# Feed-forward and output products in two 64-row parts, each beside a part of the next

## The chip, the core and the metric

One NeuronCore of a Trainium2 chip runs the whole program. Its engines work side by side and wait for each other by semaphores: TensorE (PE; its weight loads are listed as PEld), VectorE (DVE), ScalarE (ACT), GpSimdE (POOL) and the DMA queues (SP and ACT issue them here). TensorE's results land in eight PSUM banks of 128 partitions by 512 floats. The metric is the device time of one execution in microseconds (us); shown is the median of a few runs.

## What is computed

Eight sequences of 512 tokens, width 256, go through two layers:

```python
# layer 0: gated feed-forward with quantised activations and weights
h = x * (scale * rsqrt(mean(x*x) + EPS));  u = h @ up_w.T
val, gate = split(u);  h = val * gelu(gate)
x = act_quant(h) @ weight_quant(down_w).T + x
# layer 1: 16-head attention (16 wide), then SwiGLU with 1024 hidden columns;
# norm(x) = gamma * x * rsqrt(mean(x*x) + EPS) + beta
q, k, v = (norm(x) @ w.T for w in (W_q, W_k, W_v))
x = x + a_alpha * (softmax(q @ k.T / 4) @ v) @ W_o.T
y = silu(norm(x) @ gate_w.T) * (norm(x) @ hidden_w.T)
out = x + f_alpha * (y @ out_w.T + out_b)
```

## The kernel before

Phase 1 (to about 254 us) is layer 0, tile by tile. Phase 2 is layer 1, sequence by sequence ("batch" 0 to 7), and a tail finishes the last sequence. The change touches phase 2 alone.

A float32 product is made of three products of rounded parts, `PARTS = ((0, 0), (0, 1), (1, 0))`: high by high, high by low, low by high. So a feed-forward product of 128 hidden columns (`gate` f or `hidden` f, f from 0 to 7) takes 3 x 2 = 6 matmuls, since the model width is two row blocks of 128. An output piece (t, half) takes 12 matmuls of 256 columns: token tile t, one half of the sum over f.

Each batch has `HALVES` = 32 steps `h`. For each, `pe_batch` issues an excursion (`excursion_pe`): two scores (L1059) and, for a later group of heads, two raw products (L976), whose row maxima VectorE takes (L1009, `maximum_dve`) as shifts of the exponentials. Scores and raw products use 50 or 48 rows, on partitions from 0 or from 64, and a score stands beside a raw product on the other half. Every even step then has the values product (L1078) of four heads. What is left of the step is named by a table, `plan`: projections, values and attention output in steps 0 to 7; then, for the batch before, `gate` f at step 8 + 2f (`FFN_AT` = 8) and `hidden` f at step 9 + 2f; and output pieces at steps 24 to 31 (`OUT_AT` = 24). The last batch has pieces at steps 25, 27, 29 and 31 and the others behind its steps.

The other engines walk through the same table one step later (`done = table[h - 1]`). `gate_act` (ScalarE, tanh, L1311) and `gate_dve` (VectorE, L1315) read gate's bank, `product_dve` (L1322) hidden's bank, `product_act` (L1329) rounds the product to the high half `hid[0]`, and `product_pool` (GpSimd, L1333) makes the low half `hid[1]` and raises `prod_low`. In `dve_batch`, `hidden` entries are worked on ahead of the step's maximum, `gate` entries behind it. At step 25 (`SPLIT_NEXT`), in batches that have a batch after the next, ScalarE copies and GpSimd splits its input (`split_xa_act` L582, `split_xa_pool` L596); in `pool_batch` that line stands ahead of the loop over `done`. `out_pe` for half 1 waits until `prod_low` counts all eight.

Banks: scores use `psum[0:3]` in turn, and score c waits for the exponential of c - 3 (`exp_act`, L1067). `gate` and `hidden` use `ab[0]` and `ab[1]` (banks 3 and 4), output pieces of tiles 0 and 1 `ab[0]`, of tiles 2 and 3 `ab[1]`. `pair_full` and `pair_free` count their uses. Bank 5 holds the values product, 6 and 7 the raw pair. The order of all instructions is written out by these functions; an engine works through its own list in order.

## Time and profile before

| | us |
|---|---|
| median of 3 runs (lowest, highest) | 974.81 (974.50, 975.94) |
| span of the profiled execution (no other time is listed for it) | 974.5 |
| phase 2, first score to the end of batch 7's steps | 254.5 to 922.9 |
| one batch of 32 steps (batch 2) | 88.77 |
| TensorE busy in the span | 953.9 |
| VectorE, ScalarE, GpSimd busy | 719.1, 552.9, 274.1 |
| mean of one 256-column output matmul (L1347) | 0.287 |
| mean of one maximum over a raw pair (L1009) | 1.222 |

The page gives busy shares, the chain of work that ended last, and the costliest groups of instructions. A timeline row has the start in us, the length from its first start to its last end, engine and line, what is written from what, and the count; in brackets the idle time before it and what ended it. Matmuls overlap: a row of six is shorter than six times one, and a matmul whose weight load could not be hidden is recorded about 0.1 us longer. The granted TensorE clock was 0.998 in the mean (1 is full speed).

### The profile page before, as it was taken

The page shows a single profiled execution, that of the slowest core. Times are in us where ns is not written, and L with a number is a line of the kernel's source. Part 1 is how long each engine was busy: PE and PEld are TensorE (multiplying, and loading weights), DVE is VectorE, ACT ScalarE, POOL GpSimd, SP SyncE. Part 2 cuts the span into 40 slices and gives each one's busy share as a digit, 9 for nine tenths or more (in the row PEclk, how much of TensorE's full clock was granted, in tenths as well). Part 3 has the DMA queues.
Part 4 walks back from the last instruction along what each step waited for, and adds up shares of the span by engine and source line. Part 5 has one row for each costly group of instructions (what it writes and reads, how often), then busy time and mean ns, then how long its engine had stood idle before and what let it go on. Part 6 is the DMA issues. An engine that isn't in the chain of part 4 may idle for free.

```text
span 974.5 us, 15621 instructions
## 1 busy us (share of the span) xinstructions
PE 953.9 (98%) x5388; PEld 599.5 (62%) x5388; DVE 719.1 (74%) x1215; ACT 552.9 (57%) x1162; POOL 274.1 (28%) x262
## 2 busy tenths in 40 slices
PE   6999999999899999999999999999999999999998
PEld 5777777777544555655665565556546655655587
DVE  4988887999787786677677767767775777667353
ACT  5566555544666755476566547554764655466632
POOL 1366423222101223132213322231322233133242
PEclk9999999999999999999999999999999999999999
DMA  9745557434330230223022303302130212120000
GB/s 278 175 113 130 141 129 158 105 101 101 109 120 3 93 95 5 72 71 72 4 86 61 66 23 118 74 1 88 55 73 12 77 57 49 37 85 7 1 28 22
DMA packets 93741, 75.43 MB, mean 77 GB/s; under 512 B 44880, under 2 KB 79768, under 8 KB 93664
## 3 DMA queue, kind: packets, MB, share of 16 engines
q1 hardware_dynamic: 81880, 61.91, 23.5%
q10 hardware_dynamic: 11784, 12.54, 5.2%
q8 instruction: 43, 0.70, 0.3%
q14 instruction: 34, 0.28, 0.1%
HBM read 27.73 MB, written 12.61 MB: 41 GB/s over the span
## 4 chain that ended last, share of the span: by engine, by line
PE 88%; DVE 5%; issue 2%; SPq 2%; ACT 1%; DMA 1%; POOL 0%; ACTq 0%; DVEq 0%; POOLq 0%
PE bank L1303 20%; PE bank L421 13%; PE bank L1078 13%; PE bank L1059 12%; PE bank L1347 9%; PE bank L878 5%; PE raw_pair L976 5%; PE bank L937 2%; PE bank L1141 2%; DVE amax L484 2%; PE bank L331 2%; DVE h L466 1%; PE bank L339 1%; PE bank L1451 1%; DMA xk<-xT 1%
## 5 line engine op out<-in xcount | busy, mean ns | idle before, releaser
L1067 ACT ACTIVATE probs<-bank 128x512 f32<-128x512 f32 x512 | 277.8, 598 | 172.4 <-PE bank L1059 172.0
L1009 DVE TENSOR_REDUCE rowmax<-raw_pair 128x2 f32<-128x1024 f32 x225 | 274.9, 1222 | 117.4 <-PE raw_pair L976 116.4
L421 PE MATMUL bank<-up_w,xs_part 128*128 128x512 f32 x768 | 192.5, 404 | 3.9 <-POOL xs_part L403 3.9
L1059 PE MATMUL bank<-q_stack,k_stack 50*128 50x512 f32 x480 | 173.3, 447 | 0.5 <-DMA q_stack<-shift_rows 0.4
L421 PEld LDWEIGHTS bank<-up_w,xs_part 128*128 128x128 f32 x768 | 143.4, 191 | 37.8 <-POOL xs_part L403 4.7
L976 PE MATMUL raw_pair<-k_stack,q_stack 48*128 48x512 f32 x440 | 156.6, 447 | 0.0
L1333 POOL TENSOR_TENSOR hid<-scratch,hid 128x512 fp32r<-128x512 f32 x64 | 82.6, 1291 | 199.0 <-ACT hid L1329 199.0
L1078 PE MATMUL bank<-probs,v_ext 128*17 128x512 f32 x1024 | 134.8, 598 | 0.6
L1059 PEld LDWEIGHTS bank<-q_stack,k_stack 50*128 50x128 f32 x480 | 70.8, 185 | 76.5 <-issue 47.2
L1347 PEld LDWEIGHTS bank<-out_w,hid 128*128 128x128 f32 x672 | 81.4, 188 | 29.9 <-issue 29.9
L1347 PE MATMUL bank<-out_w,hid 128*128 128x256 f32 x672 | 92.0, 287 | 0.0
L1311 ACT ACTIVATE scratch<-bank 128x512 f32<-128x512 f32 x64 | 38.1, 596 | 62.6 <-PE bank L1303 59.5
L368 ACT ACTIVATE gelu<-bank,rstd 128x512 f32<-128x512 f32 x64 | 43.9, 687 | 49.2 <-PE bank L421 49.2
L976 PEld LDWEIGHTS raw_pair<-k_stack,q_stack 48*128 48x128 f32 x440 | 63.3, 185 | 4.5 <-issue 4.5
L466 DVE SCALAR_TENSOR_TENSOR h<-bank,rstd,gelu 128x512 f32<-128x512 f32 x64 | 47.7, 746 | 24.4 <-PE bank L421 22.3
L403 POOL TENSOR_TENSOR xs_part<-xs,xs_part 128x256 fp32r<-128x256 f32 x32 | 23.6, 736 | 141.1 <-DVE ms L457 120.4
L1303 PEld LDWEIGHTS bank<-xf_part,gate_w 128*128 128x128 f32 x192 | 33.5, 188 | 33.0 <-issue 27.2
L1303 PE MATMUL bank<-xf_part,gate_w 128*128 128x512 f32 x192 | 53.1, 412 | 0.0
L1315 DVE SCALAR_TENSOR_TENSOR scratch<-scratch,bank 128x512 f32<-128x512 f32 x64 | 43.3, 677 | 12.9 <-ACT scratch L1311 12.9
L1303 PE MATMUL bank<-xf_part,hidden_w 128*128 128x512 f32 x192 | 52.7, 409 | 0.0
L1303 PE MATMUL bank<-xa_part,gate_w 128*128 128x512 f32 x186 | 50.5, 407 | 0.0
L1303 PE MATMUL bank<-xa_part,hidden_w 128*128 128x512 f32 x186 | 50.1, 404 | 0.0
(196 smaller groups left out, 1328.4 us busy)
## 6 DMA issues: line engine op xcount, KB each, us to landing
q_stack<-split SPq DMA_DIRECT2D x48, 128.0 KB, 2.9
q_stack<-hid SPq DMA_DIRECT2D x42, 128.0 KB, 2.9
k_stack<-hid SPq DMA_DIRECT2D x42, 128.0 KB, 2.9
xk<-xT SPq DMA_DIRECT2D x32, 128.0 KB, 2.9
xt<-x_tok SPq DMA_DIRECT2D x32, 128.0 KB, 2.6
x_spill<-x1t ACTq DMA_DIRECT2D x32, 128.0 KB, 2.5
xa_spill<-xa ACTq DMA_DIRECT2D x32, 128.0 KB, 2.4
x_in<-xa_spill SPq DMA_DIRECT2D x8, 512.0 KB, 5.2
```

Of the source, the lines that this page charges most:

```text
L368: nc.scalar.activation(gelu[:, j, :], gate_bank[j][:], ACT.Gelu, scale=rstd[:, m % 2:m % 2 + 1]) \
L421: last = nc.tensor.matmul(bank[j][:], xs_part[a][:, m % 2, k, :], up_w[w][:, k, col + j * W:col + (j + 1) * W], start=(i == 0), stop=(i == ...
L466: nc.vector.scalar_tensor_tensor(h[:, j * W:(j + 1) * W], val_bank[j][:], rstd[:, m % 2:m % 2 + 1], gelu[:, j, :], ALU.mult, ALU.mult) \
L878: last = nc.tensor.matmul(bank[:], weight[wp][:, k, m * P:(m + 1) * P], xa_of(c)[a][:, k, :], start=(i == 0), stop=(i == 5))
L976: mm = nc.tensor.matmul(raw_pair[:, half, :], q_rows[rows, slot, qt * P:(qt + 1) * P], k_rows[rows, slot, :], start=True, stop=True)
L1009: nc.vector.reduce_max(rowmax[:, e:e + RAWS + 1:RAWS], raw_pair[:], AX.X).then_inc(raw_read, 1)
L1059: nc.tensor.matmul(score_bank[c % 3][:], k_rows[rows, slot, kt * P:(kt + 1) * P], q_rows[rows, slot, :], start=True, stop=True).then_inc(s ...
L1067: nc.scalar.activation(probs[:, (kt % 2) * J + j, :], score_bank[c % 3][:], ACT.Exp).then_inc(exp_done, 1)
L1078: last = nc.tensor.matmul(o_bank[32 * j:32 * j + HD + 1, :], v_ext[:, kt, J * g + j, :], probs[:, (kt % 2) * J + j, :], start=(kt == 0), s ...
L1303: last = nc.tensor.matmul(work_bank(n, f, spare)[:], weight[wp][:, k, f * P:(f + 1) * P], xf_of(c)[a][:, k, :], start=(i == 0), stop=(i == 5))
L1333: nc.gpsimd.tensor_tensor(hid[1][:, f, :], scratch[1][:], hid[0][:, f, :].bitcast(f32), ALU.subtract) \
L1347: last = nc.tensor.matmul(ab[m][:, (t % HALF) * D:(t % HALF + 1) * D], hid[a][:, f, t * P:(t + 1) * P], out_w[wp][:, f, :], start=(i == 0) ...
```

## The change

Feed-forward and output products are cut by rows. `hidden_lower_pe` and `out_lower_pe` issue the matmuls over partitions 0 to 63, `hidden_upper_pe` and `out_upper_pe` those over 64 to 127, into the same bank. In a step, the lower part of its table entry is issued in turns with the upper part of the step before (`beside_pe`). Step 8 has a lower part alone; one more upper part alone stands behind step 31 (in the last batch in step 24). Two semaphores, `lower_done` and `upper_done`, keep two parts out of one bank at the same time.

Since an entry is complete a step later, the other engines take `gate`, `hidden` and `out` entries two steps after the table's (`finished`). Scores have two banks; the third goes to the feed-forward products, which use banks 2, 3 and 4 in turn, and score c now waits for the exponential of c - 2. The order of output pieces is changed. The last sequence's tail is as before.

```diff
-        score_bank = psum[0:3]
+        score_bank = psum[0:2]
         ab = psum[3:5]
+        turn_bank = (psum[2], psum[3], psum[4])
...
-            pe.wait_ge(exp_done, credited(exp_done, b * 64 + (c - 2 if c >= 3 else 0)))
+            pe.wait_ge(exp_done, credited(exp_done, max(b * 64 + c - 1, 0)))
...
-            return psum[n] if spare and f % 2 == 0 else ab[n]
+            if spare:
+                return psum[n] if f % 2 == 0 else ab[n]
+            return turn_bank[(2 * f + n) % 3]
+        LOWER, UPPER = slice(0, 64), slice(64, 128)
+        def hidden_free_pe(pe, c, n, f, use):
+            if n == 0 and f > 1:
+                pe.wait_ge(pair_free[1], credited(pair_free[1], use + f - 1))
+            elif n == 0 and f == 1:
+                pe.wait_ge(pair_free[1], credited(pair_free[1], use))
+            elif n == 1:
+                pe.wait_ge(pair_free[0], credited(pair_free[0], use + f))
+        def hidden_lower_pe(pe, c, n, f, use):
+            hidden_free_pe(pe, c, n, f, use)
+            if n == 0 and f == 0:
+                pe.wait_ge(f_in_high, c + 1)
+                pe.wait_ge(f_in_copied, c + 1)
+            weight = (gate_w, hidden_w)[n]
+            for i, (a, wp, k) in enumerate([(a, wp, k) for a, wp in PARTS for k in (1, 0)]):
+                if n == 0 and f == 0 and a == 1:
+                    pe.wait_ge(f_in_low, credited(f_in_low, KD * c + (2 - k)))
+                last = nc.tensor.matmul(work_bank(n, f, False)[:], weight[wp][LOWER, k, f * P:(f + 1) * P],
+                                        xf_of(c)[a][LOWER, k, :], start=(i == 0), stop=False)
+                if i == 5:
+                    last.then_inc(lower_done, 1)
+                yield
+        def hidden_upper_pe(pe, c, n, f, use, lowers):
+            pe.wait_ge(lower_done, lowers)
+            weight = (gate_w, hidden_w)[n]
+            for i, (a, wp, k) in enumerate([(a, wp, k) for a, wp in PARTS for k in (1, 0)]):
+                last = nc.tensor.matmul(work_bank(n, f, False)[:], weight[wp][UPPER, k, f * P:(f + 1) * P],
+                                        xf_of(c)[a][UPPER, k, :], start=False, stop=(i == 5))
+                if i == 5:
+                    last.then_inc(pair_full[n], 1)
+                yield
...
+            out_free_pe(pe, t, half, use - NH)
...
+        def out_steps(half):
+            steps = [(a, wp, f) for f in range(NH) for a, wp in PARTS]
+            n = len(steps) // 2
+            return list(enumerate(steps))[half * n:half * n + n]
+        def out_half_pe(c, t, i, step, rows):
+            a, wp, f = step
+            return nc.tensor.matmul(ab[t // HALF][:, (t % HALF) * D:(t % HALF + 1) * D],
+                                    hid[a][rows, f, t * P:(t + 1) * P], out_w[wp][rows, f, :],
+                                    start=(rows == LOWER and i == 0), stop=(rows == UPPER and i == len(PARTS) * NH - 1))
+        def out_free_pe(pe, t, half, hidden_use):
+            if half == 0 and t == 0:
+                pe.wait_ge(pair_free[1], credited(pair_free[1], hidden_use + NH - 1))
+            elif half == 0 and t == HALF:
+                pe.wait_ge(pair_free[0], credited(pair_free[0], hidden_use + NH))
+        def out_lower_pe(pe, c, t, half, hidden_use):
+            out_free_pe(pe, t, half, hidden_use)
+            n = OUT_PIECES.index((t, half))
+            if n >= 2:
+                pe.wait_ge(upper_done, (len(OUT_PIECES) - 2) * c + n - 1)
+            pe.wait_ge(prod_low, credited(prod_low, c * NH + NH // 2 * (half + 1)))
+            for n, (i, step) in enumerate(out_steps(half)):
+                last = out_half_pe(c, t, i, step, LOWER)
+                if n == len(out_steps(half)) - 1:
+                    last.then_inc(lower_done, 1)
+                if n % 2 == 1:
+                    yield
+        def out_upper_pe(pe, c, t, half, lowers):
+            pe.wait_ge(lower_done, lowers)
+            for n, (i, step) in enumerate(out_steps(half)):
+                last = out_half_pe(c, t, i, step, UPPER)
+                if n == len(out_steps(half)) - 1:
+                    last.then_inc(pair_full[t // HALF] if half == 1 and t % HALF == HALF - 1 else upper_done, 1)
+                if n % 2 == 1:
+                    yield
+        def beside_pe(lower, upper):
+            for _ in range(6):
+                for half in (lower, upper):
+                    if half is not None:
+                        next(half)
+            for half in (lower, upper):
+                if half is not None:
+                    next(half, None)
...
-        OUT_PIECES = ([(0, 0)], [(2, 0)], [(0, 1)], [(1, 0)], [(1, 1)], [(2, 1)], [(3, 0)], [(3, 1)])
+        OUT_PIECES = ((0, 0), (2, 0), (0, 1), (2, 1), (1, 0), (3, 0), (1, 1), (3, 1))
...
-                    for n, pieces in enumerate(OUT_PIECES):
-                        table[OUT_AT + n] = [("out", t, half) for t, half in pieces]
+                    for n, (t, half) in enumerate(OUT_PIECES):
+                        table[OUT_AT + n] = [("out", t, half)]
...
+        LOWERS = 2 * NH + len(OUT_PIECES)
+        def finished(table, following, h):
+            before = table[h - 1] if h > 0 else []
+            skewed = ("gate", "hidden", "out") if following else ("gate", "hidden")
+            done = [p for p in (table[h - 2] if h > 1 else []) if p[0] in skewed]
+            return done + [p for p in before if p[0] not in skewed or h == HALVES]
...
+        def lower_pe(pe, b, p, u, at):
+            if p[0] == "out":
+                return out_lower_pe(pe, b - 1, p[1], p[2], u + at["hidden"])
+            return hidden_lower_pe(pe, b - 1, 0 if p[0] == "gate" else 1, p[1], u + at["hidden"])
+        def upper_pe(pe, b, p, u, at):
+            if p[0] == "out":
+                lowers = LOWERS * (b - 1) + 2 * NH + OUT_PIECES.index(p[1:]) + 1
+                return out_upper_pe(pe, b - 1, p[1], p[2], lowers)
+            n = 0 if p[0] == "gate" else 1
+            return hidden_upper_pe(pe, b - 1, n, p[1], u + at["hidden"], LOWERS * (b - 1) + 2 * p[1] + n + 1)
...
-                    elif p[0] == "out":
+                    elif p[0] == "out" and not following:
                         out_pe(pe, b - 1, p[1], p[2], u + at["out"])
                     else:
-                        hidden_pe(pe, b - 1, 0 if p[0] == "gate" else 1, p[1], u + at["hidden"])
+                        lower = lower_pe(pe, b, p, u, at)
+                        beside_pe(lower, None if h == FFN_AT else upper_pe(pe, b, table[h - 1][0], u, at))
+                if ffn and h == (HALVES - 1 if following else OUT_AT):
+                    beside_pe(None, upper_pe(pe, b, table[h if following else h - 1][0], u, at))
...
-                done = table[h - 1] if h > 0 else []
+                done = finished(table, following, h)
```

TensorE's list, step 9 and the first of step 10 of a batch: score and raw product in turns, then (before) hidden 0 in one piece:

```order
L1059 MATMUL bank<-hid 128x512
L976 MATMUL raw_pair<-k_stack,q_stack 128x512
L1059 MATMUL bank<-hid 128x512
L976 MATMUL raw_pair<-k_stack,q_stack 128x512
L1303 MATMUL bank<-xf_part,hidden_w 128x512 x6
L1059 MATMUL bank<-hid 128x512
L976 MATMUL raw_pair<-k_stack,q_stack 128x512
L1059 MATMUL bank<-hid 128x512
L976 MATMUL raw_pair<-k_stack,q_stack 128x512
L1078 MATMUL bank<-probs,v_ext 17x512 x4
```

and now, where L1322 is a lower and L1332 an upper part:

```order
L1062 MATMUL bank<-hid 128x512
L979 MATMUL raw_pair<-k_stack,q_stack 128x512
L1062 MATMUL bank<-hid 128x512
L979 MATMUL raw_pair<-k_stack,q_stack 128x512
L1322 MATMUL bank<-xf_part,hidden_w 128x512
L1332 MATMUL bank<-xf_part,gate_w 128x512
L1322 MATMUL bank<-xf_part,hidden_w 128x512
L1332 MATMUL bank<-xf_part,gate_w 128x512
```

Six matmuls over 128 rows became six over the lower 64, in turns (so on to six each) with the upper six of gate 0; the upper six of hidden 0 are in step 10.

VectorE's list from step 11 to step 14: L1009 or L1012 is the maximum, L1315 or L1360 the gate's reading, L1322 or L1367 the product; the three rows on `shift` mark step 12. Before:

```order
L1009 TENSOR_REDUCE rowmax<-raw_pair 128x2 x2
L1315 SCALAR_TENSOR_TENSOR scratch<-scratch,bank 128x512
L1322 SCALAR_TENSOR_TENSOR scratch<-scratch,bank 128x512
L1009 TENSOR_REDUCE rowmax<-raw_pair 128x2
L1015 TENSOR_SCALAR shift<-rowmax 128x16
L1017 SCALAR_TENSOR_TENSOR shift<-rowmax,shift 128x16
L1021 STREAM_TRANSPOSE shift_rows<-shift 128x32
L1009 TENSOR_REDUCE rowmax<-raw_pair 128x2
L1315 SCALAR_TENSOR_TENSOR scratch<-scratch,bank 128x512
L1322 SCALAR_TENSOR_TENSOR scratch<-scratch,bank 128x512
```

and now:

```order
L1367 SCALAR_TENSOR_TENSOR scratch<-scratch,bank 128x512
L1012 TENSOR_REDUCE rowmax<-raw_pair 128x2 x2
L1018 TENSOR_SCALAR shift<-rowmax 128x16
L1020 SCALAR_TENSOR_TENSOR shift<-rowmax,shift 128x16
L1024 STREAM_TRANSPOSE shift_rows<-shift 128x32
L1360 SCALAR_TENSOR_TENSOR scratch<-scratch,bank 128x512
L1367 SCALAR_TENSOR_TENSOR scratch<-scratch,bank 128x512
L1012 TENSOR_REDUCE rowmax<-raw_pair 128x2 x2
L1360 SCALAR_TENSOR_TENSOR scratch<-scratch,bank 128x512
```

Before, the product stood in the even step (12), ahead of its maximum, and the gate's reading in the odd one; now the gate's reading is in the even step and the product in the odd one (13), ahead of its maximum.

GpSimd's list in the later steps of a batch: L1333 or L1378 is the low half of `hid`, L596 or L598 the split of the next input, L1362 or L1456 the sum of the output. Before:

```order
L1333 TENSOR_TENSOR hid<-scratch,hid 128x512 x5
L1120 TENSOR_TENSOR split<-o_sb,split 128x512
L1333 TENSOR_TENSOR hid<-scratch,hid 128x512 x3
L596 TENSOR_TENSOR xf_part<-x_in,xf_part 128x4x2x128
L1362 TENSOR_TENSOR x<-x,scratch 128x512 x2
L1120 TENSOR_TENSOR split<-o_sb,split 128x512
```

and now:

```order
L1378 TENSOR_TENSOR hid<-scratch,hid 128x512 x5
L1123 TENSOR_TENSOR split<-o_sb,split 128x512
L1378 TENSOR_TENSOR hid<-scratch,hid 128x512 x2
L598 TENSOR_TENSOR xf_part<-x_in,xf_part 128x4x2x128
L1378 TENSOR_TENSOR hid<-scratch,hid 128x512
L1456 TENSOR_TENSOR x<-x,scratch 128x512 x2
L1123 TENSOR_TENSOR split<-o_sb,split 128x512
```

All eight low halves stood ahead of the split; now the eighth stands behind it.

## Rows read from the trace of the kernel before

**Rows 1.** The page: busy time of each engine, and the chain that ended last
```profile
PE 953.9 (98%) x5388; PEld 599.5 (62%) x5388; DVE 719.1 (74%) x1215; ACT 552.9 (57%) x1162; POOL 274.1 (28%) x262
...
PE 88%; DVE 5%; issue 2%; SPq 2%; ACT 1%; DMA 1%; POOL 0%; ACTq 0%; DVEq 0%; POOLq 0%
```

**Rows 2.** Batch 2 by windows: length, busy PE, PEld, DVE, ACT, POOL, PEclk
```profile
401.28:490.05 88.77, 88.69 (x530) 51.20 (x530) 65.03 (x89) 52.11 (x102) 23.70 (x17) 1.00 0.22 59
```

**Rows 3.** Timeline, TensorE, steps 20 and 21: start, length, count
```profile
545.96 0.49 PE L1059 MATMUL bank<-q_stack,k_stack 50*128 50x512 f32 x1
...
547.61 1.66 PE L1303 MATMUL bank<-xf_part,gate_w 128*128 128x512 f32 x6
549.19 0.50 PE L1059 MATMUL bank<-q_stack,k_stack 50*128 50x512 f32 x1
549.19 0.49 PE L976 MATMUL raw_pair<-k_stack,q_stack 48*128 48x512 f32 x1
...
549.53 0.40 PE L976 MATMUL raw_pair<-k_stack,q_stack 48*128 48x512 f32 x1
549.86 1.63 PE L1303 MATMUL bank<-xf_part,hidden_w 128*128 128x512 f32 x6
551.42 0.50 PE L1059 MATMUL bank<-q_stack,k_stack 50*128 50x512 f32 x1
```

**Rows 4.** Timeline, TensorE, output steps 25 and 26
```profile
560.13 0.49 PE L1059 MATMUL bank<-q_stack,k_stack 50*128 50x512 f32 x1
...
560.79 1.68 PE L1347 MATMUL bank<-out_w,hid 128*128 128x256 f32 x12
...
562.40 0.50 PE L1059 MATMUL bank<-q_stack,k_stack 50*128 50x512 f32 x1
...
564.04 1.65 PE L1347 MATMUL bank<-out_w,hid 128*128 128x256 f32 x12
...
565.61 0.49 PE L1059 MATMUL bank<-q_stack,k_stack 50*128 50x512 f32 x1
```

**Rows 5.** Timeline, VectorE, steps 21 and 24
```profile
549.99 1.23 DVE L1009 TENSOR_REDUCE rowmax<-raw_pair 128x2 f32<-128x1024 f32 x1 [1.13 <-PE raw_pair L976]
...
557.32 0.69 DVE L1322 SCALAR_TENSOR_TENSOR scratch<-scratch,bank 128x512 f32<-128x512 f32 x1
...
557.92 1.22 DVE L1009 TENSOR_REDUCE rowmax<-raw_pair 128x2 f32<-128x1024 f32 x1
```

**Rows 6.** Timeline, a raw product that waited for a maximum
```profile
420.78 1.21 DVE L1009 TENSOR_REDUCE rowmax<-raw_pair 128x2 f32<-128x1024 f32 x1
...
422.05 0.71 PE L976 MATMUL raw_pair<-k_stack,q_stack 48*128 48x512 f32 x2
```

**Rows 7.** Timeline, exponentials of step 7, first score of step 8
```profile
423.79 1.09 ACT L1067 ACTIVATE probs<-bank 128x512 f32<-128x512 f32 x2
...
424.30 0.50 PE L1059 MATMUL bank<-q_stack,k_stack 50*128 50x512 f32 x1
```

**Rows 8.** Timeline, ScalarE and GpSimd, steps 24 to 26
```profile
558.47 0.63 ACT L1329 ACTIVATE hid<-scratch 128x512 fp32r<-128x512 f32 x1
...
559.18 1.28 POOL L1333 TENSOR_TENSOR hid<-scratch,hid 128x512 fp32r<-128x512 f32 x1 [4.20 <-ACT hid L1329]
...
560.66 1.09 ACT L1067 ACTIVATE probs<-bank 128x512 f32<-128x512 f32 x2 [1.56 <-PE bank L1059]
...
561.64 1.06 ACT L582 ACTIVATE xf_part<-x_in 128x1024 fp32r<-128x1024 f32 x1
...
562.77 2.39 POOL L596 TENSOR_TENSOR xf_part<-x_in,xf_part 128x1024 fp32r<-128x1024 f32 x1 [2.31 <-ACT xf_part L582]
```

**Rows 9.** Timeline, TensorE at the start of phase 2
```profile
246.37 0.44 PE L339 MATMUL bank<-ident,xn 128*128 128x128 f32 x2 [1.90 <-DVE xn L360]
```

**Rows 10.** The stretch behind it by windows, columns as in rows 2
```profile
247.00:251.00 4.00, 4.00 (x12) 2.77 (x10) 2.67 (x7) 1.69 (x5) 0.97 (x2) 0.57 0.59 131
```

**Rows 11.** Timeline, weight loads of one values product
```profile
867.75 0.13 PEld L1078 LDWEIGHTS bank<-probs,v_ext 128*17 128x17 f32 x8 [0.30 <-ACT probs L1067]
```

12 lines of the change are left out of this document (6 added, 6 removed).

## The prediction

> **What bounds the kernel now.** I read the page's busy shares and chain first: TensorE is busy 98% of the span and carries 88% of the chain that ended last [rows 1]. So the kernel is as long as TensorE's list, and the question is what each entry costs and who else comes close behind.
>
> The change touches phase 2. It runs eight batches of 32 steps (the loop variable `h`). Each step computes two scores and two raw products (an *excursion*, 64-row parts), every even step adds a values product, and from step 8 on comes one *slot*: six 512-column feed-forward matmuls, or twelve 256-column output matmuls. A batch takes 88.77 us, 88.69 of them TensorE busy, at full clock [rows 2]. Its timeline gives an even feed-forward step 549.19 - 545.96 = 3.23 us and an odd one 551.42 - 549.19 = 2.23 [rows 3]; in the output stage 3.21 (562.40 to 565.61) and 2.27 (560.13 to 562.40) [rows 4].
>
> Inside a slot the pitch is about 0.23 us: six matmuls cover 1.63, the last is 0.40 long, the first gap is like the one inside an excursion (0.34, from 549.19 to 549.53), so (1.63 - 0.40 - 0.34) / 4 = 0.22 to 0.23 [rows 3]. For 256 columns, twelve matmuls cover 1.68 and one is 0.29 long; with a first gap 0.11 longer than the others that gives (1.68 - 0.29 - 0.11) / 11 = 0.117 [rows 4]. Where 64-row and 128-row work meet, the next start comes 0.33 late (549.53 to 549.86), and the gap after it is 0.34 again: against two pitches of 0.23, one **switch** costs 0.20 us. An odd step has two switches, an even one three (the values product stands between two more).
>
> VectorE is close behind. In the odd step its maximum starts at 549.99 and runs 1.23, to 551.22; the next raw product starts at 551.42 [rows 3, 5]. There is one pair of raw banks, so this loop cannot be shorter than: second raw product to maximum 0.46 (549.53 to 549.99), the maximum 1.22, 0.06 until a raw product that waits for it starts (420.78 + 1.21 = 421.99, start 422.05) [rows 6], and 0.34 to the second one: 2.08 us, though TensorE's own list could be shorter.
>
> **Part 1: switches that go.** Slots now consist of 64-row parts like the excursions: a lower part beside the upper part of the slot before. In pairs two parts start together, as the score and raw product do (both 549.19, both 549.53) [rows 3]. No row shows a long series of pairs. Below, I bound the pair's pitch by the 0.23 of full matmuls; above, by the 0.34 between the two pairs of an excursion. I take 0.23, because full matmuls show the same 0.34 right behind a switch and 0.23 after it. Then:
> - an even step loses the switch at its end: 3.23 becomes 3.02, 3.21 becomes 3.00. Twelve a batch: -2.6 us.
> - an odd step loses both: 8 x 0.23 = 1.84 for TensorE. VectorE does not let it be that short. The step's results are now read one step later, so the product of scratch and hidden bank (0.69, start to next start 0.60: 557.32 to 557.92) stands ahead of the **odd** step's maximum and gate's reading, about as long, in the even one. The upper part of `hidden` ends with the even step: its last matmul starts 0.23 before the odd step, and a reader of a bank starts 0.46 after a raw product's start and about 0.05 more where it has two waits (an estimate), so product at +0.29, maximum at +0.90 to +2.12, raw product's load at +2.17, product effective at +2.28. Step 11 to 25: 2.27 against 2.23 to 2.27, some +0.1 a batch together; step 9, with no product yet, takes the bound 2.08: -0.17.
> - the Trainium skill has a rule against this change (TensorEngine Tiling (Array Packing), Performance Considerations, PSUM Bottleneck): tiling makes TensorE faster, not the emptying of PSUM. By it the odd steps gain nothing, which is what rows 3 and 5 give with their own numbers; without it they would give 0.4 each.
> - output steps 27 and 29: 2.27 to 2.08, -0.38.
>
> **Part 2: the slot more.** A pipeline of lower and upper parts needs one slot more: the last upper part runs beside nothing, 12 x 0.117 = 1.40. Step 31 becomes 2 x 0.23 + 1.40 + 1.40 = 3.26, that is +0.99. VectorE's slack of 0.2 in step 31 is used up inside that.
>
> **Part 3: two score banks.** A score now waits for the exponential two before it. Nearly everywhere that has ended long before. Not in step 8: ScalarE does three affine passes in step 6 and 7, its two exponentials run from 423.79 to 424.88, and the scores of step 8 start at 424.30 and 0.34 later [rows 7]. The second must wait until 424.94 and then shows its weight load (0.11): +0.40 a batch. Third banks of the slots (freed by the product of f - 2 and the gate's reading of f - 1) are free a step before they are wanted: 0.
>
> Sum of these for each of batches 1 to 6: -2.6 + 0.1 - 0.17 - 0.38 + 0.99 + 0.40 = -1.7 us.
>
> **Part 4: a new wait, and what stands ahead of it.** GpSimd's list changes its order. Before, the eighth low half of `hid` (1.28) stands in step 24, ahead of the split of the next batch's input (2.39). Now it moves to step 25, where the split is written first. The split waits for ScalarE's copy (1.06), which now stands behind ScalarE's high half of the eighth product (0.63) [rows 8]. In step 25, counted from its start: exponentials 0.42 to 1.50 (560.66 - 560.13 = 0.53, less the load of 0.11 that a switch exposes), product_act 1.42 to 2.05, copy to 3.1, split 3.2 to 5.55, low half to 6.85. TensorE waits for exactly this (`prod_low` = 8) ahead of output piece (0, 1) in step 26. It would be there at 2.27 + 1.64 - 0.11 = 3.8 (values and switch: 562.40 to 564.04 [rows 4]) and gets going at 7.0: a stall of **3.2 us**. All output parts, the next scores and raw products are queued behind it, and nothing after gives it back, since TensorE's list is the bound. The split exists in batches 1 to 5 (batches 6 and 7 load no further input): +16 us.
>
> A stall can cost clock. Before 246.37 TensorE was idle 1.90 us [rows 9], and from 247 to 251 the granted clock was 0.57 in the mean, mostly the lower of the two levels, 1.2 GHz [rows 10]: 4 x 0.43 = 1.7 us of full speed lost. The new stalls are longer, but full work stands before and behind. Bounds 0 and 1.7 each; I take 0.8, since the one like row fell and part of a slow stretch may lie in the stall: +4.
>
> **The ends.** Batch 7 keeps the old output pieces: -1.8 for eight even steps, +1.4 for the last upper part alone, the score wait at steps 6 and 8 of 0.5 each, and at three output steps 0.4 each (an estimate after step 8), less 0.3 in step 23, which has no maximum: +1.5. Batch 0, only score waits in its first steps: +0.3, bounds 0 and 0.8.
>
> **Sum.** 6 x (-1.7) + 16 + 4 + 1.5 + 0.3 = +12. The profiled span is 974.5 us and the median 974.8, so 0.3 lies around the span. Forecast: **987 us**, 1.2% slower.
>
> **Rivals.**
> 1. *Odd steps follow TensorE.* The stalls are there, but the odd steps come down to 1.84. Against my forecast that is 0.43 for eight steps and 0.24 for three, -4.2 a batch, -25 in all; with no clock lost, 987 - 29 = 958. Mechanism: VectorE starts product and maximum as soon as data lands, and raw products get ahead of it. It decides from a gain of 2.7 us a batch, which pays the stalls (16 / 6). Against it: the 2.08 loop. If only the product's place is harmless and the loop holds (0.19 x 8 x 6 = 9), and the clock stays up, 987 - 13 = 974, no change. Chances 0.15 and 0.08.
> 2. *Pairs are dearer.* If each 512-column pair costs the 0.34 seen in the excursion, a feed-forward slot takes 2.0 instead of 1.38: each of 16 steps +0.4 to +0.6 against the forecast, 50 us or more in all, near 1040. For it: every excursion shows 0.34 between its pairs. Against it: the slots' own first gap. Chance 0.06. A mild form, twelve pairs of 256 columns where two lower parts go ahead of two upper ones, costs 0.15 in an even output step: +4, inside the range.
> 3. *The list of instructions feeds too slowly.* An output slot has 24 matmuls and 24 loads in 1.40 us. In the values product eight weight loads fit into 0.13 us of busy time [rows 11], so loads that are queued go at once; a slower feed of 58 ns each (the pace at which full 256-column matmuls with their loads go, 0.117 / 2) would make an output slot 2.8 and the kernel some 55 us longer, near 1040. Chance 0.04. The Trainium skill (TensorE: Matmul & The Clock Gate, Part 2) gives about 62 ns for a MATMUL where the sequencer's own code decodes it. By that an output slot would be an estimated 1.49, and the sum 4 us more; no row here tells which decoding is on.
> 4. *The stall is not there,* because the low half is early enough: 987 - 20 = 967. The order of the list speaks against it: two waits on one in-order engine. Chance 0.04.
>
> **How the numbers follow.** The forecast's own case has 0.63, with 980 to 996: from no clock lost and a milder product (983, then -3) to every clock lost and dearer output pairs (+4.5 and +4). Low end 970 reaches into rivals 1 and 4, high end 1000 leaves out most of 2 and 3. A difference under 0.2% cannot be told from none by this measurement (the three runs lie 0.15% apart). Faster: rival 1's first form and rival 4, 0.19; same 0.08; slower the rest, 0.73.
>
> **What the profile would show.** Odd feed-forward steps of 2.25 to 2.3 with TensorE waiting for the maximum, even ones of 3.0; a pitch of 0.23 in pairs; in five batches a wait for `hid`'s low half at step 26 of some 3 us, with the POOL split right before it; PEclk below 1.0 behind some of those; step 31 near 3.3. I am wrong if TensorE does not wait for GpSimd there, or if the odd steps are under 2.1.

## The result, and the profile after

The changed kernel takes 1010.1 us in the median of four runs (1006.49 to 1014.74), against 974.65 for the kernel before on the same chip (974.25 to 975.94): a ratio of 1.036, 95% interval 1.0327 to 1.0393. That is slower, as forecast, but by 35 us and not by 12; the forecast of 987 and its upper end of 1000 were both too low. The profiled execution took 1006.49 us for a span of 1004.7, so it is 30.2 us of span that the traces can explain; the other runs are longer as their granted clock is lower: the longest has a mean of 0.981 where this one has 0.990, and 0.009 of its span is 9 us, while the two spans lie 8 us apart.

The page of the changed kernel, busy time and chain, against [rows 1]:

```profile
PE 960.3 (96%) x6636; PEld 640.8 (64%) x6636; DVE 729.3 (73%) x1215; ACT 552.9 (55%) x1162; POOL 273.4 (27%) x262
...
PE 77%; DVE 11%; ACT 4%; issue 2%; POOL 2%; SPq 2%; DMA 1%; ACTq 0%; DVEq 0%; POOLq 0%
```

TensorE's share of the chain fell from 88% to 77%, VectorE's rose from 5% to 11%, and GpSimd is in it. Batches 2, 5 and 6 by windows (length, busy PE, PEld, DVE, ACT, POOL, PEclk), against [rows 2]:

```profile
405.20:498.87 93.67, 89.87 (x723) 57.75 (x721) 66.07 (x89) 52.09 (x102) 23.56 (x18) 0.98 0.21 56
683.16:775.28 92.12, 88.36 (x723) 56.53 (x722) 66.05 (x89) 52.08 (x102) 23.54 (x18) 1.00 0.21 57
775.28:864.51 89.23, 88.30 (x723) 56.35 (x721) 66.88 (x89) 51.37 (x101) 21.26 (x17) 1.00 0.20 54
```

Before, every loop batch took 88.77 us, with 0.1 us of it not PE. Now 3.8 us of batches 2 and 5 are idle, and 0.9 of batch 6, which has no split of a next input. Counted from first score to first score, batches 1 to 5 are 3.4 to 4.9 us longer (19.5 together), batch 6 0.5, batch 7 10.5; the rest moves by -0.2. Four things make this up.

**The stall of step 26** is as forecast. Batch 4, timeline (start, length, engine, line, count, idle time before):

```profile
663.45 1.06 ACT L584 ACTIVATE xa_part<-x_in 128x1024 fp32r<-128x1024 f32 x1
...
664.58 2.35 POOL L598 TENSOR_TENSOR xa_part<-x_in,xa_part 128x1024 fp32r<-128x1024 f32 x1 [5.01 <-ACT xa_part L584]
666.89 1.26 POOL L1378 TENSOR_TENSOR hid<-scratch,hid 128x512 fp32r<-128x512 f32 x1
668.30 1.66 PE L1403 MATMUL bank<-out_w,hid 64*128 64x256 f32 x24 [2.85 <-POOL hid L1378]
```

GpSimd splits the next input for 2.35 us while TensorE waits for the low half behind it. The same wait stands in batches 1 to 5. Against [rows 8] the order of the two GpSimd instructions is reversed.

**A held VectorE in step 20** is not in the forecast. Batch 4, timeline:

```profile
648.79 1.28 POOL L1123 TENSOR_TENSOR split<-o_sb,split 128x512 fp32r<-128x512 f32 x1 [0.98 <-ACT split L1119]
...
648.89 1.21 DVE L1018 TENSOR_SCALAR shift<-rowmax 128x16 fp32r<-128x16 f32 x1
...
650.14 0.17 DVE L1020 SCALAR_TENSOR_TENSOR shift<-rowmax,shift 128x16 fp32r<-128x16 f32 x1
...
650.48 0.65 DVE L1360 SCALAR_TENSOR_TENSOR scratch<-scratch,bank 128x512 f32<-128x512 f32 x1
...
651.18 0.50 PE L1322 MATMUL bank<-xa_part,hidden_w 64*128 64x512 f32 x1 [0.56 <-DVE scratch L1360]
```

The shift's first operation, on 16 numbers a partition, lasts from 648.89 to 650.10: until GpSimd's subtraction ends at 650.07. Gate's reading comes late, and the next lower part waits for its bank. In the kernel before, the same two rows of the same step (it starts at 634.72) stand the other way round, and the shift is done before the subtraction starts:

```profile
636.99 0.17 DVE L1015 TENSOR_SCALAR shift<-rowmax 128x16 fp32r<-128x16 f32 x1
...
637.52 1.29 POOL L1120 TENSOR_TENSOR split<-o_sb,split 128x512 fp32r<-128x512 f32 x1 [4.65 <-ACT split L1116]
```

Counted from the start of the step, the shift moved from 2.27 to 2.61 us and the subtraction from 2.80 to 2.51, since ScalarE no longer makes a high half ahead of its copy in this step.

How general the hold is, the whole trace shows. Of the 32 instructions of L1018, 24 take 174 to 177 ns, and the eight that start beside a GpSimd operation 1210 to 1234; each ends 29 to 32 ns after that operation. The same holds for the division's product (L1105): 24 of 32 take 424 to 426 ns, the eight beside GpSimd 1318 to 1335. VectorE's readers of PSUM are not held: the maximum is 1.22 us with GpSimd and without. Nor is every operation on SBUF: in the kernel before, seven transposes of `o_pair` (L1110) start beside a low half and take 699 to 700 ns, as the others do. The Trainium skill has this rule (SBUF — State Buffer, Who interferes with whom): VectorE and GpSimd share a pair of SBUF ports as an exclusive lock, and whoever comes second is blocked until the first ends. The trace agrees for the operations that are held here; the prediction never asked the question.

**The last batch** lost twice. Its raw groups end in the odd steps 13 and 21 (a pause at step 5 shifts them), where the shift now stands behind product and maximum and meets GpSimd: two operations in step 13, one in step 21. In the kernel before, the groups ended in the same odd steps, but no product stood ahead; there the shift of step 13 was free (0.17 us), and steps 15 and 16 took 2.27 and 3.24 us, as in the other batches. Steps 13 to 16 of batch 7 now:

```profile
901.50 0.69 DVE L1367 SCALAR_TENSOR_TENSOR scratch<-scratch,bank 128x512 f32<-128x512 f32 x1 [0.84 <-PE bank L1332]
...
903.27 1.28 POOL L1378 TENSOR_TENSOR hid<-scratch,hid 128x512 fp32r<-128x512 f32 x1 [2.82 <-ACT hid L1374]
903.35 1.23 DVE L1018 TENSOR_SCALAR shift<-rowmax 128x16 fp32r<-128x16 f32 x1
...
904.51 1.28 POOL L1191 TENSOR_TENSOR x_in<-wo,aalpha 128x512 f32<-128x512 f32 x1
904.62 1.21 DVE L1020 SCALAR_TENSOR_TENSOR shift<-rowmax,shift 128x16 fp32r<-128x16 f32 x1
...
906.10 3.53 SPq L1030 DMA_DIRECT2D q_stack<-shift_rows  x6
...
911.24 0.47 PE L1062 MATMUL bank<-q_stack,k_stack 50*128 50x512 f32 x1 [1.76 <-DMA q_stack<-shift_rows]
```

Step 16's score waits for rows that VectorE turned at 905.86, and step 24's once more (2.10 us, to 935.51).

**The clock** falls behind some of these waits, from 2.4 to 1.2 GHz. Windows behind a stall of batch 1 (granted 0.51), behind that of batch 3 (1.00) and behind the wait at 935.51 (0.51):

```profile
390.10:393.60 3.50, 3.50 (x35) 3.34 (x34) 1.23 (x1) 1.08 (x2) 0.00 (x0) 0.51 0.02 5
...
576.00:580.00 4.00, 3.84 (x56) 3.69 (x56) 1.23 (x1) 1.09 (x2) 0.01 (x1) 1.00 0.00 0
936.30:943.20 6.90, 6.90 (x27) 4.57 (x20) 2.00 (x4) 2.46 (x5) 1.04 (x1) 0.51 0.00 0
```

In this execution two of the five stalls of step 26 cost clock, 3.4 us at half speed each, and both waits of batch 7 did (3.4 and 6.8).

### The profile page after: what moved, and what is told of

Read it like the earlier page. It is cut to its first block, busy times and chain, and to the rows that moved or that the text cites. A ratio compares the mean times of both kernels' runs of the same rounds, so it can differ in the third digit from the quotient of the medians.

```text
span 1004.7 us, 18048 instructions
## 1 busy us (share of the span) xinstructions
PE 960.3 (96%) x6636; PEld 640.8 (64%) x6636; DVE 729.3 (73%) x1215; ACT 552.9 (55%) x1162; POOL 273.4 (27%) x262
## 4 chain that ended last, share of the span: by engine, by line
PE 77%; DVE 11%; ACT 4%; issue 2%; POOL 2%; SPq 2%; DMA 1%; ACTq 0%; DVEq 0%; POOLq 0%
PE bank L423 14%; PE bank L1081 11%; PE bank L1322 10%; PE bank L1062 8%; PE bank L1403 7%; PE raw_pair L979 5%; PE bank L881 4%; DVE rowmax L1012 3%; PE bank L1332 3%; PE bank L940 2%; PE bank L1144 2%; PE bank L1348 2%; PE bank L333 2%; DVE amax L486 1%; PE bank L1391 1%
## 5 line engine op out<-in xcount | busy, mean ns | idle before, releaser
L1012 DVE TENSOR_REDUCE rowmax<-raw_pair 128x2 f32<-128x1024 f32 x225 | 275.0, 1222 | 109.9 <-PE raw_pair L979 109.0
L1378 POOL TENSOR_TENSOR hid<-scratch,hid 128x512 fp32r<-128x512 f32 x64 | 81.8, 1279 | 232.1 <-ACT hid L1374 232.1
L979 PE MATMUL raw_pair<-k_stack,q_stack 48*128 48x512 f32 x440 | 136.1, 445 | 1.5 <-DVE rowmax L1012 1.5
L1062 PEld LDWEIGHTS bank<-q_stack,k_stack 50*128 50x128 f32 x480 | 82.6, 187 | 45.2 <-ACT probs L1070 25.0
L1403 PEld LDWEIGHTS bank<-out_w,hid 64*128 64x128 f32 x1152 | 84.0, 191 | 37.8 <-issue 34.8
L1403 PE MATMUL bank<-out_w,hid 64*128 64x256 f32 x1152 | 90.1, 286 | 14.3 <-POOL hid L1378 14.2
L1367 DVE SCALAR_TENSOR_TENSOR scratch<-scratch,bank 128x512 f32<-128x512 f32 x64 | 43.7, 683 | 28.2 <-PE bank L1332 26.2
L1332 PE MATMUL bank<-xf_part,hidden_w 64*128 64x512 f32 x192 | 55.3, 423 | 0.0
L1322 PEld LDWEIGHTS bank<-xf_part,gate_w 64*128 64x128 f32 x192 | 33.8, 189 | 32.5 <-issue 27.6
L1322 PE MATMUL bank<-xf_part,gate_w 64*128 64x512 f32 x192 | 54.2, 416 | 0.0
L1360 DVE SCALAR_TENSOR_TENSOR scratch<-scratch,bank 128x512 f32<-128x512 f32 x64 | 43.0, 672 | 12.7 <-ACT scratch L1356 12.7
L1322 PE MATMUL bank<-xf_part,hidden_w 64*128 64x512 f32 x192 | 49.9, 393 | 1.8 <-DVE scratch L1360 1.8
L1332 PE MATMUL bank<-xf_part,gate_w 64*128 64x512 f32 x192 | 50.2, 394 | 0.0
```

Source lines behind the costliest of these rows:

```text
L979: mm = nc.tensor.matmul(raw_pair[:, half, :], q_rows[rows, slot, qt * P:(qt + 1) * P], k_rows[rows, slot, :], start=True, stop=True)
L1012: nc.vector.reduce_max(rowmax[:, e:e + RAWS + 1:RAWS], raw_pair[:], AX.X).then_inc(raw_read, 1)
L1062: nc.tensor.matmul(score_bank[c % 2][:], k_rows[rows, slot, kt * P:(kt + 1) * P], q_rows[rows, slot, :], start=True, stop=True).then_inc(s ...
L1322: last = nc.tensor.matmul(work_bank(n, f, False)[:], weight[wp][LOWER, k, f * P:(f + 1) * P], xf_of(c)[a][LOWER, k, :], start=(i == 0), st ...
L1332: last = nc.tensor.matmul(work_bank(n, f, False)[:], weight[wp][UPPER, k, f * P:(f + 1) * P], xf_of(c)[a][UPPER, k, :], start=False, stop= ...
L1378: nc.gpsimd.tensor_tensor(hid[1][:, f, :], scratch[1][:], hid[0][:, f, :].bitcast(f32), ALU.subtract) \
```

## The experiments

**1. GpSimd's low half ahead of the split**

```
 for p in done:
     if p[0] == "hidden":
         product_pool(pool, b - 1, p[1])
     ...
+if following > 1 and h == SPLIT_NEXT:        # was ahead of the loop
+    split_xa_pool(pool, b + 2)
```

> The changed kernel, with one thing turned round on GpSimd in step 25 of batches 1 to 5: the low half of the eighth hidden product first, the split of the next input behind it. Theory (the stall of step 26 is nothing but the split standing ahead of that low half): steps 26 and 27 of batches 1 to 5 come down from 8.3 us together to the 5.35 of batch 6, which has no split: 5 x 2.95 = -14.7 us, and the two stretches at half clock that followed such stalls in the profiled run (3.4 us each at 0.5, 1.7 us of full speed lost in each) go as well: -18 in all, 992 against 1010. Rival A (the low half is late anyway, since ScalarE's high half is late): -5 or less. Rival B (the split, now 1.3 us later, makes the next batch's projections wait): the first steps of batches 2 to 6 get longer by up to 1.3 us each, -10 to -12 in all.

Measured: 991.85 us (988.96 to 993.61), ratio to the kernel before 1.0178 (1.0156 to 1.02). Batches 1 to 6 take 88.95 to 89.2 us, all alike. In a batch of it the low half, then the split, then an unhindered TensorE:

```profile
652.23 1.29 POOL L1378 TENSOR_TENSOR hid<-scratch,hid 128x512 fp32r<-128x512 f32 x1 [4.05 <-ACT hid L1374]
...
653.47 2.58 POOL L598 TENSOR_TENSOR xa_part<-x_in,xa_part 128x1024 fp32r<-128x1024 f32 x1
...
653.97 1.66 PE L1403 MATMUL bank<-out_w,hid 64*128 64x256 f32 x24
```

The order of two instructions on an engine that is busy 27% of the span was worth 18 us: the theory's number, and half of the loss. Neither rival holds: the stall is gone whole, and the first steps of batches 2 to 6 are as long as in the changed kernel (4.96 us for step 0).

**2. Normalise two steps later**

```
-if g == 2 and h % 8 == 4:    # ScalarE's copy and GpSimd's subtraction
+if g == 2 and h % 8 == 6:
```

> The changed kernel with the normalise step of the first pair of head groups (ScalarE's copy and GpSimd's subtraction, step 20) two steps later, in step 22. Theory (a small VectorE operation on SBUF is held as long as a GpSimd operation runs: the shift's first operation takes 1210 to 1229 ns beside GpSimd's subtraction instead of 175, and the gate's reading, the next lower part and so TensorE wait): the first shift operation of step 20 is back at some 0.2 us, steps 20 and 21 come down from 6.42 to 5.35, in batches 1 to 6: -1.0 each, -6 in all, 1004 against 1010. Rival A (the 1.2 us are a wait of the operation that the profile books as its duration, and it stays wherever GpSimd's operation is): the operation is still 1.2 us long and the time is unchanged. Rival B (step 20 is long because VectorE has maximum, three shift operations and the gate's reading there, whatever GpSimd does): 6.42 falls by 0.2 at most.

Measured: 1006.27 us (1004.92 to 1008.2), ratio 1.0321 (1.0304 to 1.0338). Step 21 is 1.86 us long in all seven batches where it was 2.7 in six: -0.85 each, -5 in all, where -1.0 and -6 were expected. Steps 20 and 21 take 5.57 us and not the 5.35 of the other pairs; these 0.2 are what is left to rival B. The median shows 4; the granted clock of these runs is 0.980 to 0.985, that of the changed kernel's 0.981 to 0.990, and in the profiled execution all five stalls cost clock. Step 20 of batch 4, where VectorE's shift now has no GpSimd beside it, and GpSimd's subtraction two steps on:

```profile
647.50 0.17 DVE L1018 TENSOR_SCALAR shift<-rowmax 128x16 fp32r<-128x16 f32 x1
...
648.06 0.65 DVE L1360 SCALAR_TENSOR_TENSOR scratch<-scratch,bank 128x512 f32<-128x512 f32 x1
...
652.81 1.29 POOL L1123 TENSOR_TENSOR split<-o_sb,split 128x512 fp32r<-128x512 f32 x1 [0.83 <-ACT split L1119]
```

Nothing of VectorE's own was changed: it was GpSimd that held it.

**3. and 4. The last batch: no pause, or shift ahead of product**

```
-LAST_PAUSE = 5                                        # 3
+LAST_PAUSE = HALVES
...
-elif p[0] == "hidden":                                # 4, on VectorE
+elif p[0] == "hidden" and not (not following and h in (13, 21)):
+...                                                   # these two: behind maximum and shift
```

> The changed kernel, with the pause of the raw products at step 5 of the last batch taken out: its raw groups end in the even steps 12 and 20, as in the other batches, and no longer in the odd steps 13 and 21. Theory (the last batch lost 9 us because the shift now stands behind product and maximum in an odd step and its rows reach the stacks too late for the scores of steps 16 and 24, each wait being followed by a stretch at half clock): the waits in steps 15 and 24 go, steps 15 and 16 come down from 9.4 to about 5.4, and the rest of the batch keeps its clock: the batch 87.8 -> 79 to 81, -7 to -9 in all, 1002 against 1010; step 5 may get longer by some tenths of a us. Rival A (what takes the time is the row cut itself in that batch, with its whole output products beside cut ones): no more than -2. Rival B (the transfers of the shift's rows wait for something else, as their queue): the scores still wait in steps 16 and 24, -2 to +1.

Measured: 1000.65 us (994.21 to 1003.98), ratio 1.0254 (1.0208 to 1.03): -9.5, with runs that lie 10 us apart. The traces are surer: batch 7 takes 79.67 us where it took 87.80, -8.1. Step 15 takes 1.86 us where it took 4.71, step 16 3.48 for 4.70. Both rivals fall.

> The changed kernel; in steps 13 and 21 of the last batch VectorE makes maximum and shift ahead of the product and not behind it. Theory (order on VectorE: the shift leaves 0.6 us earlier, and may then also miss GpSimd's low half, beside which its two small operations took 1.2 us each instead of 0.2): the shift's rows are turned 0.6 to 2.5 us earlier, the score of step 16 waits that much less: -1 us if only the order counts, -5 to -7 if the hold by GpSimd goes too and the clock stays up; the product of these steps is late, +0.3 to +0.6 in the step behind each. Rival (only the place of the group's end counts, an odd step instead of an even one): within 1 us of the changed kernel.

Measured: 1001.36 us (998.81 to 1003.86), ratio 1.0269 (1.0247 to 1.0292): -9, more than I expected of it; batch 7 takes 79.21 us, -8.6. With the shift ahead of the product it starts before GpSimd's low half (which needs that product) and cannot be held:

```profile
909.01 0.17 DVE L1018 TENSOR_SCALAR shift<-rowmax 128x16 fp32r<-128x16 f32 x1
...
909.22 0.18 DVE L1020 SCALAR_TENSOR_TENSOR shift<-rowmax,shift 128x16 fp32r<-128x16 f32 x1
909.43 0.21 DVE L1024 STREAM_TRANSPOSE shift_rows<-shift 128x32 f32<-128x32 f32 x1
909.57 0.66 DVE L1367 SCALAR_TENSOR_TENSOR scratch<-scratch,bank 128x512 f32<-128x512 f32 x1
...
914.49 0.46 PE L1062 MATMUL bank<-q_stack,k_stack 50*128 50x512 f32 x1 [0.17 <-DMA q_stack<-shift_rows]
```

The rival (only the place of the group's end counts) falls: with the end still in an odd step, the wait goes from 1.76 us to 0.17.

**5. The three together**

> The three edits of the first experiments together in the changed kernel: low half ahead of the split in step 25, normalise in step 22, no pause of the raw products in the last batch. Theory (stalls of step 26, holds of VectorE by GpSimd and the late shift rows of the last batch are all of the loss, and add up): loop batches of 89.2 - 0.9 = 88.35 us against 88.77 before the change (-0.4 each, six of them), the last batch 1.4 us longer than before the change (87.8 less 8.2 for the pause and 0.9 for the hold is 78.7, against 77.3), +0.3 at the end: 974 us, within 0.2% of the kernel before the change. Rival (part of the loss comes back, since a transfer or an engine that a stall had covered is late next): a loop batch stays above 89, 979 or more.

Measured: 977.23 us (twelve runs, 974.62 to 980.94) beside 976.03 of the kernel before (17 runs), ratio 1.0015 (1.0003 to 1.0027). Loop batches 88.49 us (88.14 for the first), batch 7 78.67. So the kernel with the three edits is 0.15% slower than the kernel before, and the three causes make up nearly the whole loss. This is the bare change: cutting the rows, freed of what it ran into, gains 2.1 us in the six loop batches, and the last batch gives 1.4 of it back. The 1.2 us of the medians do not show this gain; what stands ahead of phase 2 varies by more from trace to trace (it starts at 259.68 here, at 251.0 to 259.7 in all), so I compare batch lengths.

**6. and 7. Why so little: half the maximum, in the mended kernel and in the kernel before**

```
-nc.vector.reduce_max(rowmax[...], raw_pair[:], AX.X)
+nc.vector.reduce_max(rowmax[...], raw_pair[:, :, 0:256], AX.X)
```

> The kernel with the three edits, and VectorE's maximum in the loop batches reads only 256 of the 512 columns of each raw product (half of the numbers are left out of the maximum, so the shift of the scores is another). The maximum takes some 0.65 us instead of 1.22. Theory (VectorE's loop holds the pairs of feed-forward steps at 5.35 us, TensorE's own list would be 3.02 + 1.84 = 4.86): pairs of steps fall to 4.86 to 4.95, some eight pairs a batch, -0.45 each: -3.5 us a batch, -24 in all, 950 against 974. Rival (the cut work has dearer pairs or switches on TensorE than taken, and the loop is not the bound): less than -5 us.

Measured: 947.72 us (947.28 to 950.09), ratio 0.9717 (0.9702 to 0.9732): 29.5 us less than in experiment 5, where 24 was expected; a loop batch takes 83.96 us. Three feed-forward steps of it:

```profile
607.89 0.39 PE L1062 MATMUL bank<-q_stack,k_stack 50*128 50x512 f32 x1
...
608.22 0.69 DVE L1367 SCALAR_TENSOR_TENSOR scratch<-scratch,bank 128x512 f32<-128x512 f32 x1 [1.38 <-PE bank L1332]
608.83 0.69 DVE L1012 TENSOR_REDUCE rowmax<-raw_pair 128x2 f32<-128x512 f32 x1
...
609.75 0.39 PE L1062 MATMUL bank<-q_stack,k_stack 50*128 50x512 f32 x1
...
612.77 0.39 PE L1062 MATMUL bank<-q_stack,k_stack 50*128 50x512 f32 x1
```

Odd 609.75 - 607.89 = 1.86, even 612.77 - 609.75 = 3.02: to 0.02 what the prediction made of TensorE's own list (8 x 0.23 and 3.23 less a switch). The shorter maximum has a side effect: none of the 32 division products (L1105) is held by GpSimd here, 13 are in experiment 5. The pair of steps 26 and 27, where that hold may count, fell by 0.3 us, 2 of the 29.5 us in all.

> The kernel before the change, and VectorE's maximum in the loop batches reads only 256 of the 512 columns of each raw product (half of the numbers are left out of the maximum). Theory (before the change TensorE's own list sets every step; VectorE's loop ends beside it and holds nothing): an odd feed-forward step keeps its 2.23 to 2.25 us, 974 +- 2 us; the cut kernel with the same edit is then 27 us faster than this one, which is what cutting the rows is worth to TensorE alone. Rival (the odd steps were already held by the maximum, and the cut of the rows gained its time from VectorE's slack): odd steps of 2.0 or less, 970 or less, above 950.

Measured: 974.7 us (ten runs) beside 975.45, ratio 0.9992 (0.9982 to 1.0001): no change, odd steps 2.23 to 2.25. So the cut, with its slot more and its two score banks, is worth 27 us to TensorE (the two kernels differ in the last batch's pause too), and in the real kernel VectorE's loop around the maximum keeps nearly all of it.

**8. The product behind the maximum in odd steps**

```
-elif p[0] == "hidden":                  # ahead of the maximum
+elif p[0] == "hidden" and not (p[1] < NH - 1):
     product_dve(...)
 ...                                     # maximum, shift, gate_dve
+elif p[0] == "hidden" and (p[1] < NH - 1):
+    product_dve(...)
```

> The kernel with the three edits, and VectorE takes the product of scratch and hidden bank in odd steps behind the maximum and no longer ahead of it (the eighth stays ahead, since output work waits for it soon). Theory (what holds an even and an odd feed-forward step together at 5.35 us is the loop product, maximum, next raw products; TensorE's own work would take less): without the product in it the loop is 0.46 + 1.22 + 0.06 + 0.34 = 2.08 us in an odd step, and the pair of steps takes 3.02 + 2.08 = 5.10: -0.25 for seven pairs in each of seven batches, -12 us, 962 against 974. Rival A (the loop is not it, a pair of steps takes 5.35 us of TensorE's own time): unchanged. Rival B (the product, now 0.6 us or more later, delays ScalarE's tanh and the exponentials, and with two score banks the scores wait): pairs of steps of 5.3 to 5.6, 0 to +10 us.

Measured: 967.38 us (966.27 to 970.17), ratio 0.9919 (0.9904 to 0.9934): faster than both kernels. Expected was 962; the gain is 10 us and not 12. Two pairs of steps take 10.2 us where they took 10.7 (steps 12 to 15: 3.24 + 2.04 + 3.09 + 1.86, in the kernel of experiment 5 3.48 + 1.86 + 3.50 + 1.86), a loop batch 86.9. The pair of steps 18 and 19 did not gain (5.4 us). Maximum first, product behind it, and the next raw product waits less:

```profile
605.47 1.23 DVE L1012 TENSOR_REDUCE rowmax<-raw_pair 128x2 f32<-128x1024 f32 x1 [1.19 <-PE raw_pair L979]
606.61 0.68 DVE L1367 SCALAR_TENSOR_TENSOR scratch<-scratch,bank 128x512 f32<-128x512 f32 x1
...
606.75 0.53 PE L979 MATMUL raw_pair<-k_stack,q_stack 48*128 48x512 f32 x2
```

The wait of the raw products' loads for a maximum, from the waits by line (total us, times, longest), of the kernel of experiment 5 and of this one:

```profile
PEld raw_pair L979 <- DVE rowmax L1012: 22.5, 54, 0.6
```

```profile
PEld raw_pair L979 <- DVE rowmax L1012: 8.0, 40, 0.6
```

The kernel with half the maximum has no such entry.

**9. Output products whole**

```
-LOWERS = 2 * NH + len(OUT_PIECES)
+LOWERS = 2 * NH
...
-elif p[0] == "out" and not following:
+elif p[0] == "out":
     out_pe(...)              # 128 rows, read one step later
```

> The kernel with the three edits, and the output products of batches 0 to 5 whole again (128 rows, read one step later), so that only the feed-forward products are cut; the last upper part of these runs alone in step 24. Theory (by the steps so far): steps 24 to 31 are 5.33 + 5.35 + 5.15 + 6.37 = 22.2 us with cut output; whole they are 3.2 + 1.4 (the upper part alone) + 2.27 + 3 x 5.47 = 23.3: +1.1 us a batch, six of them, +7 in all, 981. Rival (the cut output work, with its slot more, is the part of the change that costs): faster by 1 to 5 us.

Measured: 980.95 us (979.77 to 981.99), ratio 1.0055 (1.0038 to 1.0071); a loop batch is 89.6 us for 88.49, +1.1 as worked out. The medians lie only 3.7 us apart and not 7, as the expectation's 981 was counted from 974 and experiment 5 gave 977.23. The last upper part has to run alone somewhere; once the feed-forward products are cut, cutting the output too costs less than not. It showed where one unforeseen term is from as well: step 0 is 4.60 us here and 4.98 in the kernel of experiment 5, so that +0.35 (4.63 before the change) comes from the last output part behind it.

**10. Two score banks alone, in the kernel before**

```
-score_bank = psum[0:3]      # c % 3, waits for the exponential c - 3
+score_bank = psum[0:2]      # c % 2, waits for the exponential c - 2
```

> The kernel before the change with two score banks in turn and not three, nothing else. Theory as forecast (the scores of step 8 wait for exponentials that ScalarE's affine passes made late): +0.40 us a batch there, seven batches, +3 to +3.5 in all with what batch 7 and batch 0 add: 978. Rival (the wait is small, as in the changed kernel, whose step 7 is 0.15 longer and whose step 8 is no longer than before): +0.1 to +0.15 a batch, +1 in all, 976.

Measured: 979.46 us (978.76 to 980.74), ratio 1.0044 (1.0029 to 1.0059). A loop batch is 89.17 for 88.77, +0.40, in step 7 and 8 only; batch 7 +1.6. Step 8 of batch 5:

```profile
689.80 1.09 ACT L1067 ACTIVATE probs<-bank 128x512 f32<-128x512 f32 x2
690.46 0.18 PEld L1059 LDWEIGHTS bank<-q_stack,k_stack 50*128 50x128 f32 x1 [0.51 <-ACT probs L1067]
...
690.94 0.18 PEld L1059 LDWEIGHTS bank<-q_stack,k_stack 50*128 50x128 f32 x1 [0.30 <-ACT probs L1067]
```

The forecast's number stands and the rival falls; the changed kernel pays this too (in its batch 5 the loads of step 8's scores wait 0.50 and 0.30 us for exponentials). Both scores of the step wait, not the second alone.

## Why the prediction was wrong

The failed steps are two terms of the sum. "6 x (-1.7)" took every VectorE operation at its free length and left out some small terms: the traces give +2.4. "+1.5" for batch 7 took its shifts to arrive as early as before: the traces give +10.5. The stall and VectorE's loop, the two mechanisms that the forecast rested on, are there. In spans, us:

| term | forecast | traces |
|---|---|---|
| batches 1 to 6, parts 1 to 3 | -10.2 | +2.4 (bare change -2.1, held shifts +4.5) |
| stalls and their clock | +20 | +17.5 |
| batch 7 | +1.5 | +10.5 |
| batch 0 and the rest | +0.3 | -0.2 |
| sum | +11.6 | +30.2 |

The 5 us from here to the median's +35.5 go with the lower clock of the other runs. Point by point:

- **What bounds the kernel, and the pair's pitch.** Right. TensorE before (experiment 7), pairs at 0.23 (experiment 6: an odd step of 1.86). Rival 2 (dearer pairs) and rival 3 (feed too slow) are out; an output slot of 24 matmuls takes 1.38 us (662.00 to 663.37 in the changed kernel), less than the 1.49 that rival 3's last sentences worked out.
- **Part 1, odd steps held by VectorE.** Right in the mechanism, near in size: pairs of steps take 5.35 us in steps 12 to 19 where 2.27 + 3.02 = 5.29 was forecast. The forecast signs, 2.27 and 3.0, do not appear: counted by first scores it is 1.86 and 3.49, since the first score does not wait for a maximum and only the raw product does. So the prediction's own sign of being wrong, odd steps under 2.1, came true although the loop holds; it was a badly chosen sign, as only the sum of a pair tells. Rival 1 would need a shorter maximum (experiment 6 gives its 1.86), and its mild form a product in another place (experiment 8 is that). Steps 27 and 29: 5.1 for the pair (28, 29) is right, (26, 27) is 5.38 and not 5.08. There the division's product is held by GpSimd's low half in the kernel of experiment 5 (1342 ns for 425); half a maximum brings the pair down to 5.08, but no run took that hold away alone.
- **Part 2, the slot more.** 3.23 + 1.89 + 3.27 + 3.16 = 11.55 in steps 28 to 31 against 11.34: +0.2. Step 0, +0.35, was left out.
- **Part 3, score banks.** +0.40 a batch, right (experiment 10).
- **Parts 1 to 3 as a sum.** -1.7 a batch was forecast; -0.3 came (experiment 5). The 1.4 between, from the step lengths: seven pairs (steps 12 to 25) 0.6, of which step 20 has 0.3; pair (26, 27) 0.3; steps 28 to 31 0.2; step 0 0.35; the steps 6 to 11 give 0.3 back, and 0.2 is rounding. Over six batches this is 8.5 us.
- **Part 4, the stall.** Right: 16 + 4 forecast, 18 measured when it was taken away (17.5 in the traces), 2.95 us for 3.2 in each batch, with clock lost in two of five.
- **What failed: VectorE's durations taken as fixed.** The forecast moved operations of ScalarE, GpSimd and VectorE by a step and asked only who waits for them, not who then runs beside whom. In step 20 it was GpSimd's subtraction that met the shift, which came 0.34 us later and it 0.29 earlier. The row of a held operation was in the trace of before too: L1017 took 1137 to 1143 ns in five of 32, where 174 is usual, and hid it in slack. In the changed kernel the hold costs 0.85 us a batch in step 21 (experiment 2).
- **What failed as much: the last batch as a copy of the others.** "+1.5" is what comes out once the group ends lie in even steps (+1.4, experiment 5); as built, the odd group ends, the product ahead of the shift and GpSimd beside it made it 10.5. By experiments 3 and 4 each of two edits takes 9 to 9.5 us away, 8.1 and 8.6 by the length of the batch. The lists that the forecast was made from show VectorE's order in a loop batch, where the shift stands in the even step 12; that the last batch has product and shift in one odd step follows from its pause at step 5, and was not looked at.

Sum of the profiled difference, each from the batch lengths of two traces: stalls with their clock +17.5 (batches 1 to 5, changed kernel less experiment 1), held shifts +4.5 (batches 1 to 6, experiment 1 less experiment 5), last batch +9.1 (changed kernel less experiment 5), the bare change -2.1 in the loop batches and +1.4 in the last, -0.2 in the rest: +30.2.

## What to carry to other kernels

A change that delays readers by a step moves work on every engine: list, for each engine, what it now starts beside what, and not only who waits for whom. An in-order engine that is busy a quarter of the time can own half of a loss by the order of two instructions. And when a busy engine is freed, look for the loop of the next one (here the product ahead of the maximum): its order decides whether anything is gained; the mended kernel with that order is 0.8% faster than the kernel before, the change alone 3.6% slower.

## What the runs showed of the hardware

- Some VectorE operations on SBUF, even very small ones, are held for the whole rest of a GpSimd operation: the shift's (TENSOR_SCALAR of one SBUF input, SCALAR_TENSOR_TENSOR of two, 16 numbers a partition) take up to 1234 ns and not 175 in the changed kernel, ending 29 to 32 ns behind it; the division's product (TENSOR_TENSOR of two SBUF inputs) takes up to 1335 and not 425, ending 280 to 283 ns behind it. Not held are the operations with an operand in PSUM (maximum 1.22 us, gate's reading 0.68) and the transposes from SBUF to SBUF (0.70).
- TensorE's two halves of rows take their matmuls apart from each other. In program order a step has score, raw product (upper rows), score (upper), raw product (lower). Where the raw products waited, both start together and the score between them 0.34 us later:

```profile
635.57 0.40 PE L1062 MATMUL bank<-q_stack,k_stack 50*128 50x512 f32 x1
...
635.91 0.50 PE L979 MATMUL raw_pair<-k_stack,q_stack 48*128 48x512 f32 x2
...
636.25 0.40 PE L1062 MATMUL bank<-q_stack,k_stack 50*128 50x512 f32 x1
```

  Who waits for the last raw product is released only after that score: the maximum of such a step starts 0.80 us behind the raw products' start (630.55 to 631.35) and not 0.46. That completions are told in program order is my reading of it; no run tried it by itself.
- A stall of 2.9 us with full work on both sides costs clock sometimes (two of five in the changed kernel's trace, two, four and five of five in those of experiments 3, 4 and 2), 3.4 or 6.8 us at 1.2 GHz; what decides it stays open.
